# Edge ranks from TensorE products in place of 20 scans, and tiles 0 to 3 normed on their own, in the first block of a graph-transformer kernel

## The reference

```python
xn = layernorm(x)
W = einsum('rb,bio->rio', comp, basis)            # 8 relation matrices out of 4 bases
H = einsum('ni,rio->nro', xn, W)                  # rows of h_table
agg = segment_sum(H[src, etypes], dst, 2500)      # message passing
out = agg + xn @ loop_weight + bias
q, k, v = split(xn @ Wqkv.T + bqkv)               # and then an attention of its own
```

## Time and profile before

| | |
|---|---|
| median of 3 runs | 2431.36 us (2429.86 to 2431.77) |
| the profiled execution, first to last instruction | 2432.3 us |
| TensorE busy | 2103.5 us (86%) |
| VectorE busy | 1491.2 us (61%) |
| GpSimd busy | 974.7 us (40%) |
| ScalarE busy | 737.7 us (30%) |
| mean granted TensorE clock | 0.952 of full |
| first block, `slots_and_dense` | 0 to 138.6 us |
| second block, `front0` | 139.8 to 391.9 us |

### The profile page before, as it was taken

How to read it: one execution, slowest core, us unless ns; L and a number is a source line. 1 busy time by engine, 2 the same in 40 slices (tenths; PEclk the granted TensorE clock), 3 DMA queues, 4 the chain that set the end, 5 groups by cost and what they waited for, 6 DMA issues and landing times. The chain is left out here.

```text
span 2432.3 us, 31951 instructions
## 1 busy us (share of the span) xinstructions
PE 2103.5 (86%) x9692; PEld 1341.8 (55%) x9692; DVE 1491.2 (61%) x2938; ACT 737.7 (30%) x1962; POOL 974.7 (40%) x976
## 2 busy tenths in 40 slices
PE   4869996888899898699959958888887889999999
PEld 2346663444444446566636536666666766565665
DVE  8997777777787865433345558888887761211211
ACT  2511111111111113033312245555554232323232
POOL 4900004777666650055540067777776320000000
PEclk9989998999999998599979979999999989999999
DMA  3012223333333353433341178888888300000000
GB/s 113 31 59 98 98 93 95 103 102 102 95 94 95 94 75 102 156 53 57 57 102 44 44 210 243 240 239 239 239 240 199 113 1 1 9 9 1 9 9 8
DMA packets 118886, 241.54 MB, mean 99 GB/s; under 512 B 23255, under 2 KB 73182, under 8 KB 116030
## 3 DMA queue, kind: packets, MB, share of 16 engines
q0 software_dynamic: 56640, 160.17, 25.3%
q1 hardware_dynamic: 62078, 79.33, 10.1%
HBM read 196.24 MB, written 43.19 MB: 98 GB/s over the span
## 5 line engine op out<-in xcount | busy, mean ns | idle before, releaser
L672 POOL DMA_INDIRECT rows<-h_table,row_rel x372 | 361.4, 971 | 409.3 <-POOLq L95 268.1
L2137 PE MATMUL p_ag<-rows_g,oh_g 128*128 128x260 f32 x1488 | 398.7, 408 | 77.7 <-issue 57.6
L1980 POOL DMA_INDIRECT rows_g<-g_table,row_src x372 | 352.8, 949 | 255.1 <-POOLq L95 142.1
L2137 PEld LDWEIGHTS p_ag<-rows_g,oh_g 128*128 128x128 f32 x1488 | 256.9, 192 | 107.7 <-issue 74.3
L2503 DVE SCALAR_TENSOR_TENSOR x<-p_yf,cw_f,x 128x256 f32<-128x256 f32 (+1 forms) x160 | 66.4, 477 | 278.6 <-PE p_yf L2663 278.6
L927 PE MATMUL p_agg<-rows,oh 128*128 128x256 f32 x744 | 194.9, 396 | 24.8 <-DVE x L723 24.8
L2030 DVE TENSOR_TENSOR rows_g<-rows_g,p_e 128x2048 f32<-128x2048 f32 x93 | 211.8, 2278 | 0.0
L927 PEld LDWEIGHTS p_agg<-rows,oh 128*128 128x128 f32 x744 | 131.5, 190 | 88.6 <-DVE x L723 41.9
L792 DVE TENSOR_TENSOR fT<-a_sb,p_sel 128x512 f32<-128x512 f32 x200 | 128.6, 684 | 74.5 <-ACT a_sb L888 43.0
L2663 PE MATMUL p_yf<-f,h_f 128*128 128x256 f32 (+1 forms) x640 | 145.7, 381 | 0.8 <-ACT h_f L2555 0.8
L2613 PE MATMUL p_1f<-qT,f 128*128 128x512 f32 (+1 forms) x320 | 143.2, 591 | 0.5 <-ACT qT L2531 0.5
(11 more groups left out here) (434 smaller groups left out, 3535.8 us busy)
## 6 DMA issues: line engine op xcount, KB each, us to landing
h_table<-h_out SPq DMA_DIRECT2D x20, 1024.0 KB, 4.2
where_g<-d_table SPq DMA_DIRECT2D x93, 128.0 KB, 4.3
w<-in_L_ffn_W SPq DMA_DIRECT2D x16, 512.0 KB, 8.8
rows<-h_table,row_rel POOLq DMA_INDIRECT x372
rows_g<-g_table,row_src POOLq DMA_INDIRECT x372
g_table<-row SPq DMA_DIRECT2D x20, 260.0 KB
f<-in_L_ffn_W SPq DMA_DIRECT2D x16, 256.0 KB, 5.9
xT_table<-xT SPq DMA_DIRECT2D x20, 128.0 KB, 1.7
```

The lines of the kernel that those rows point to most:

```text
L672: pool.indirect_dma_start(rows[:, r, j], None, st.h_rows, bass.IndirectOffsetOnAxis(ap=st.row_rel[:, at:at + 1], axis=0)).then_inc(gathere ...
L1980: pool.indirect_dma_start(rows[:, r, j], None, st.g_table, bass.IndirectOffsetOnAxis(ap=st.row_src[:, at:at + 1], axis=0)).then_inc(gather ...
L2137: last = pe.matmul(p_a[:, k % NS, h, 0:HALF], oh[:, r, j], rows[:, r, j, h * HALF:(h + 1) * HALF], start=j % SUP == 0, stop=j % SUP == SUP ...
```

## The change

The loads are put in another order: x's first group, dst, the weights, then the other edge numbers and the rest of x. Tiles 0 to 3 are normed alone; the others follow after the edge work. `hot` is written by 20 instructions in place of one. The rank of an edge within its tile and column comes from a TensorE product with a triangle of ones (`before`, with 49152 on its diagonal, so that the edge's own tile has the largest value), to which a second product adds the start of that tile and column (`spread` times `start_h`). VectorE takes the maximum over the 20 tiles (`pos`). Counts come from 20 products (`count`), prefix sums over tiles from one (`prefix`, now at t = 3). The 32 instructions on `w_rel` stand between the maxima. GpSimd builds the constants for that, and its 20 additions of `b_v` to v go to the second block.

```diff
+MARK = 49152.0
+SPREAD = 32 + T
+CQ = T - 1
+PREFIX_AT = 3
+TILES_AT = 5
...
+            load_x(0)
+            sp.dma_start(dst_i[:, :], io["dst"].rearrange("(p c) -> p c", p=EP)).then_inc(dst_in, 16)
+            sp.dma_start(w_lv[:, :, 0:D], io["L0_gnn_loop_weight"].rearrange("(k p) o -> p k o", p=P)).then_inc(w_in, 16)
+            sp.dma_start(w_lv[:, :, D:], io["wqkv0"][:, 2 * D:].rearrange("(k p) o -> p k o", p=P)).then_inc(w_in, 16)
+            sp.dma_start(w_qk[:, :, :], io["wqkv0"][:, 0:2 * D].rearrange("(k p) o -> p k o", p=P)).then_inc(w_in, 16)
             sp.dma_start(src_i[:, :], io["src"].rearrange("(p c) -> p c", p=EP)).then_inc(edges_in, 16)
             sp.dma_start(et_i[:, :], io["edge_type_8"].rearrange("(p c) -> p c", p=EP)).then_inc(edges_in, 16)
-            for g in range(NG - 1):
-                sp.dma_start(st.x[:, g * GT * D:(g + 1) * GT * D].rearrange("p (t d) -> p t d", d=D),
-                             io["x"][g * GT * P:(g + 1) * GT * P, :].rearrange("(t p) d -> p t d", p=P)).then_inc(x_in[g], 16)
+            for g in range(1, NG - 1):
+                load_x(g)
...
+            pool.affine_select(out=spread[:, :, :], in_=spread[:, :, :], compare_op=ALU.not_equal, fill=1.0,
+                               base=0, pattern=[[-1, T], [0, EP]], channel_multiplier=1).then_inc(made, 1)
+            pool.wait_ge(made, 8)
+            pool.affine_select(out=spread[:, :, :], in_=spread[:, :, :], compare_op=ALU.not_equal, fill=float(SUP * P),
+                               base=-32, pattern=[[-1, T], [0, EP]], channel_multiplier=1).then_inc(spread_made, 1)
...
+            pool.wait_ge(b_in, 16)
+            for t in range(T):
                 pool.wait_ge(lv_used, t + 1)
-                pool.wait_ge(xn_ready, t + 1)
                 x = st.x[:, t * D:(t + 1) * D]
                 pool.tensor_tensor(x, x, loop_p[:, t % 2], ALU.add).then_inc(loop_added, 1)
-                v = v1_t[:, :, t * (DH + 1):t * (DH + 1) + DH]
-                pool.tensor_tensor(v, v, b_v[:, :].rearrange("p (h e) -> p h e", h=H), ALU.add).then_inc(v_added, 1)
-
-            def add_qk(t):
                 pool.wait_ge(qk_used, t + 1)
                 part = qk_t[:, :, t * DH:(t + 1) * DH]
-                pool.tensor_tensor(part, part, b_qk[:, :].rearrange("p (g e) -> p g e", g=2 * H), ALU.add).then_inc(v_added, 1)
-
-            pool.wait_ge(w_in, 80)
-            for t in range(T):
-                add_lv(t)
-                add_qk(t)
+                pool.tensor_tensor(part, part, b_qk[:, :].rearrange("p (g e) -> p g e", g=2 * H), ALU.add).then_inc(qk_added, 1)
...
+            norm(0, GT)
+            dve.wait_ge(dst_in, 16)
+            link(dve.tensor_scalar(e_i[:, :], dst_i[:, :], 7, None, ALU.logical_shift_right))
+            scaled(0, GT, 1)
+            link.inc(dve.tensor_scalar(dst_i[:, :], dst_i[:, :], P - 1, None, ALU.bitwise_and))
+            link(dve.tensor_copy(e_tile[:, :], e_i[:, :]))
+            for t in range(T):
+                last = dve.tensor_scalar(hot[:, t], e_tile[:, :], float(t), None, ALU.is_equal)
+                if t % GT == GT - 1:
+                    last.then_inc(tile_hot_ready, 1)
+
+            dve.wait_ge(edges_in, 32)
...
+            norm(GT, T)
+            scaled(GT, T, 2)
...
-            link(dve.tensor_tensor(hot[:, :, :], e_tile[:, :].unsqueeze(1).broadcast_to([EP, T, EC]),
-                                   iota_t[0:EP, :].unsqueeze(2).broadcast_to([EP, T, EC]), ALU.is_equal))
-            link(dve.tensor_reduce(tcount[:, :], hot[:, :, :], AX, ALU.add))
-            dve.sem_inc(counted, 1)
...
+            count = p_c[0:SPREAD, 0:EC]
+            dve.wait_ge(counted, 1)
+            link(dve.tensor_reduce(tcount[:, :], count, AX, ALU.add))
+            link(dve.tensor_scalar(need_i[:, :], tcount[:, :], float(SUP * P - 1), None, ALU.add))
             link(dve.tensor_scalar(need_i[:, :], need_i[:, :], 8, None, ALU.logical_shift_right))
             link(dve.tensor_copy(need[:, :], need_i[:, :]))
-            link(dve.tensor_tensor_scan(cum[:, :], ones_t[:, :], need[:, :], 0.0, ALU.mult, ALU.add))
-            link(dve.tensor_tensor(cum[:, :], cum[:, :], need[:, :], ALU.subtract))
-            link(dve.tensor_scalar(base[:, :], cum[:, :], float(SUP * P), -1.0, ALU.mult, ALU.add))
-            link(dve.tensor_tensor(base[0:EP, :], base[0:EP, :], p_t[0:EP, 1, 0:T], ALU.add))
-
-            link(dve.tensor_tensor(cmp_s, cum[0:1, :].unsqueeze(1).broadcast_to([1, NSUP, T]),
-                                   sup_i[:, :].unsqueeze(2).broadcast_to([1, NSUP, T]), ALU.is_le))
-            link(dve.tensor_reduce(tos[:, :], cmp_s, AX, ALU.add))
-            link(dve.tensor_scalar(st.tile_of[:, 0:NSUP], tos[:, :], -1.0, None, ALU.add))
-
+            dve.sem_inc(need_ready, 1)
+            link.inc(dve.tensor_tensor_scan(scan[:, :], ones_e[:, :], count, 0.0, ALU.mult, ALU.add))
+            dve.wait_ge(prefixed, 1)
+            link.inc(dve.tensor_copy(cum[:, :], p_s[0:SPREAD, 0:1]))
+            link(dve.tensor_scalar(base[:, :], p_s[0:SPREAD, 0:1], float(SUP * P), None, ALU.mult))
+            link.inc(dve.scalar_tensor_tensor(out=start_i[:, :], in0=scan[:, :], scalar=base[:, 0:1], in1=count, op0=ALU.add, op1=ALU.subtract))
+            link(dve.tensor_scalar(begun[:, :], st.iota_s[0:T, 0:NSUP], cum[0:T, 0:1], None, ALU.is_ge))
+            dve.sem_inc(begun_ready, 1)
+            link.inc(dve.tensor_scalar(start_i[0:32, :], start_i[0:32, :], SUP * P - 1, None, ALU.bitwise_and))
+            link(dve.tensor_scalar(start_i[32:, :], start_i[32:, :], 8, None, ALU.logical_shift_right))
+            link(dve.tensor_copy(start_h[:, :], start_i[:, :]))
+            dve.sem_inc(start_ready, 1)
...
+            dve.wait_ge(tiles_found, 1)
+            dve.tensor_scalar(st.tile_of[:, 0:NSUP], p_c[0:1, 0:NSUP], -1.0, None, ALU.add).then_inc(tiles_taken, 1)
+            dve.wait_ge(basis_in, 16 * (NB + 2))
+            done = 0
             for t in range(T):
-                link.inc(dve.tensor_tensor_scan(scan[:, t], ones_e[:, :], hot[:, t], base[0:EP, t:t + 1], ALU.mult, ALU.add))
-            dve.wait_ge(dv, link.base + link.k)
-            link(dve.tensor_tensor(scan[:, :, :], scan[:, :, :], hot[:, :, :], ALU.mult))
-            link(dve.tensor_reduce(e_a[:, :], scan[:, :, :].rearrange("p t c -> p c t"), AX, ALU.add))
-            link(dve.tensor_copy(dst_i[:, :], e_a[:, :]))
+                dve.wait_ge(slots_put, t + 1)
+                if t == 0:
+                    link.inc(dve.tensor_copy(pos[:, :], p_s[0:EP, 0:EC]))
+                else:
+                    link.inc(dve.tensor_tensor(pos[:, :], pos[:, :], (p_s, p_c)[t % 2][0:EP, 0:EC], ALU.max))
+                dve.wait_ge(dv, link.base + link.k)
+                dve.sem_inc(slots_taken, 1)
+                if t % 2:
+                    for n in range(done, done + 3):
+                        relation(n)
+                    done += 3
+            link(dve.tensor_scalar(dst_i[:, :], pos[:, :], -MARK, None, ALU.add))
...
-                link.inc(dve.tensor_tensor_scan(scan[:, t], ones_e[:, :], hot[:, t], base[0:EP, t:t + 1], ALU.mult, ALU.add))
-            dve.wait_ge(dv, link.base + link.k)
-            link(dve.tensor_tensor(scan[:, :, :], scan[:, :, :], hot[:, :, :], ALU.mult))
-            link(dve.tensor_reduce(e_a[:, :], scan[:, :, :].rearrange("p t c -> p c t"), AX, ALU.add))
...
+            def count():
+                pe.wait_ge(consts, NCONST)
+                for t in range(T):
+                    if t % GT == 0:
+                        pe.wait_ge(tile_hot_ready, t // GT + 1)
+                    last = pe.matmul(p_c[0:SPREAD, 0:EC], col_at[:, CQ - t:CQ - t + SPREAD], hot[:, t], start=t == 0, stop=t == T - 1)
+                last.then_inc(counted, 1)
...
+            def tiles():
+                pe.wait_ge(begun_ready, 1)
+                pe.wait_ge(start_ready, 1)
+                pe.matmul(p_c[0:1, 0:NSUP], ones_e[0:T, 0:1], begun[:, :], start=True, stop=True).then_inc(tiles_found, 1)
+
+            def put(t):
+                if t >= 2:
+                    pe.wait_ge(slots_taken, t - 1)
+                elif t:
+                    pe.wait_ge(tiles_taken, 1)
+                out = (p_s, p_c)[t % 2][0:EP, 0:EC]
+                pe.matmul(out, before[0:EP, 0:EP], hot[:, t], start=True, stop=False)
+                pe.matmul(out, spread[:, t], start_h[:, :], start=False, stop=True).then_inc(slots_put, 1)
...
+                if t == 1:
+                    count()
                 if t == PREFIX_AT:
                     prefix()
+                if t == TILES_AT:
+                    tiles()
+                    pe.wait_ge(spread_made, 1)
+                if TILES_AT <= t < TILES_AT + T // 2:
+                    put(2 * (t - TILES_AT))
+                    put(2 * (t - TILES_AT) + 1)
...
+        @block.gpsimd
+        def _(pool):
+            pool.wait_ge(st.b_v_in, 16)
+            for t in range(T):
```

(70 more changed lines are left out.)

128 lines of the change are left out of this document (62 added, 66 removed).

## The result

The changed kernel runs in 2414.4 us (median of 4 runs, 2409.39 to 2417.55), the kernel before in 2431.6 beside it: ratio 0.9924, 95% interval 0.9911 to 0.9938, 17 us. Repeated on another chip, with six runs, it is 0.9904 [0.9887, 0.9921], 22 us. The forecast was 2409, 22 us under; the first measurement lies 5.4 us above it, inside 2404 to 2416. The profiled execution was the fastest of its four, with a span of 2407.7 (clock 0.958), 24.6 under the span before.

The account below looks back on a forecast made before the run. VectorE was taken to end the first block, TensorE's 3.66 us per tile being the next bound; 33.8 us gained less 11.8 lost in `front0` gives 22.0, so 2409 us (2404 to 2416, 53%), with bounds 2393 to 2419.

Parts of the forecast that it names:

- the first block's gain: First block: `front0` starts at 106.0 in place of 139.8, 33.8 us earlier.
- the loss in `front0`: Second block: moved v additions and a slow clock make it 11.8 us later; bounds nothing and 14.
- TensorE from 11.5: First block: x lands at 6.5, `rstd` of tiles 0 to 3 at about 10, TensorE's tile 0 from 11.5.
- `hot` complete at 23, written in 12 us: First block: GpSimd's constants hold up the 20 `hot` rows, complete at 23 (bounds 14.5, 28), written in 12 rather than 4.4.
- need_ready at 34, TensorE there at 33: First block, ahead of tile 3: VectorE is ready 11 us behind `hot`, at 34; TensorE's tiles 1 and 2 end at 33.
- The rest, 68.7: First block: 17 tiles x 3.66, ten pairs of puts x 0.6, about 0.5 extras: 68.7 us, TensorE done at 103.
- Behind TensorE, GpSimd's last qk addition; VectorE idle from about 93: First block's end: GpSimd's addition to qk is last, at about 105; VectorE is idle from about 93 until then.
- hots(0) in turns, 18.5: Start of `front0`: GpSimd's 20 v additions alternate with VectorE's first 20 `hots` instructions, which take 18.5 us.
- rival "no turns": In `front0`, comparisons keep GpSimd out: loss 0 to 2 us, time 2398; chance 20%.
- 2.7 us for a slow clock: In `front0`, after TensorE's idle gap, 5.4 us of products run at half the clock at first, adding 2.7 us.
- TensorE's clock as the way to a slower kernel: First block: waits for `slots_taken` leave tiles at 1.2 GHz, 3.65 us more each, 2471 with all 17; chance 3%.
- the outermost rivals: 2392: constants don't delay `hot` (10%), combined with no turns. Upper: selects of 4.7 each (12%), 2414, up to 2419.

Follow-up runs that it names:

- run 3: Changed kernel with GpSimd's two selects on `spread` behind tile 0's additions and `iota_h` behind tile 9's; ratio 0.9905 to the kernel before.
- run 6: Changed kernel, first select waiting for `recs_split`, given as VectorE's last edge-number copy was issued, and `iota_h` behind tile 9; ratio 0.9904 to the kernel before.
- run 9: Changed kernel, selects after `rec_lo` is written, `iota_h` behind tile 9, v additions in the first block (tiles 0 to 3 four tiles late); ratio 0.9846 to the kernel before.
- run 10: Changed kernel, selects after `rec_lo` is written, `iota_h` behind tile 9, each v addition in `front0` waiting for a one-hot group; 2397.25 us, ratio 0.9835 to the kernel before.
- run 1: Changed kernel with GpSimd's addition to v of tile t waiting for `front0`'s one-hot group t + 1; ratio 0.9867 to the kernel before.
- run 4: Changed kernel with 40 additions to v in `front0`: 20 that add `b_v`, 20 that subtract it; ratio 0.9924 to the kernel before.
- run 2: Changed kernel with the additions to v back in the first block and `b_v` loaded after `b_qk`; ratio 0.9878 to the kernel before.
- run 7: Changed kernel with run 6's placing of the constants and the additions to v back in the first block; ratio 0.9883 to the kernel before.

## Why the prediction was right, and where its steps were not

The total came out: 2409 forecast, a ratio of 0.991, between the two measurements. Two errors of the sum nearly cancel: the first block's gain was put 5.0 us too high, the loss in `front0` 3.4 too high, and 22.0 became 20.4. That they cancel is luck. By its steps:

- *TensorE from 11.5*: **wrong, 17.1**. x landed earlier than assumed (4.76, not 6.5). The prediction charged the constants to `hot`; they fell on the work ahead of it. It held one-input f16 and int32 operations at risk and let the seven small operations of the norm run free. The rows after show L312, L315 and `e_i` held for 9.1 us, and runs 3, 6, 9 and 10, with the constants elsewhere, show TensorE starting at 8.7 to 8.8. The Trainium skill ("SBUF — State Buffer", section "Who interferes with whom") names both kinds: an instruction with two SBUF inputs against a GpSimd instruction that reads, and one in a two-port mode against any; with one input outside these modes there is no contention. The traces agree: two-input `mean` is held by a select, and one-input statistics go on at 0.33 beside one (run 6). Whether the held one-input operations (L315, `e_i`) ran in a two-port mode no trace shows.
- *`hot` complete at 23, written in 12 us*: complete at 20.3, written in 3.23, so this sign of being right did not come. TensorE did not wait, as it was late itself. The price of a select (2.2) was 2.47.
- *need_ready at 34, TensorE there at 33*: 32.5 and 33.8, no wait. The times are right, the way to them is not. In the forecast TensorE started at 11.5 and then stood from 17.7 to 23 for `hot`, 5.3 us. In fact it started 5.6 us later and never stood. The constants cost about what the forecast took them to cost (6.6 us at tile 3; runs 6, 9 and 10, without them, start front0 5.6 to 6.2 us earlier), through another wait; that the two are equal is luck. The 10 us for tiles 1 and 2 were 10.5: two tiles of 3.7 at the full clock and 3.1 for the count, where the prediction speaks of a slow clock.
- *The rest, 68.7*: **mis-sized, 74.2**. A pair of puts was priced at 0.6 from the 0.16 of `p_rec` products, and measured 1.15, ten times: 5.5 us, all of the first block's error. The number of products was right, their price was not: up to 0.29 for 340 columns, twice that of the count's of the same width.
- *Behind TensorE, GpSimd's last qk addition; VectorE idle from about 93*: right (109.87; 94.07).
- *hots(0) in turns, 18.5*: right in kind, 16.4 in size; comparisons go at 0.66 each, not 0.75. The clock near 0.5 as `p_rec` starts came too (0.50 from 124 to 127.5). Runs 1 and 4 settle it: without additions 3.93 for 17, with 40 the second group is as slow as the first. The rival "no turns" is out.
- *2.7 us for a slow clock*: 1.4 (6.96 against 5.54). TensorE's 9.0 us of idleness cost that much in this execution; it cost 2.0 in the repeat (7.54).
- *TensorE's clock as the way to a slower kernel*: it did not come; no put waited for `slots_taken`, and the clock stood at 1.00 from 41 to 108.
- *Slips in the working*, none of which moves the total: the select's own figures (0.17 and 0.9 ns a column) give 2.4 for 2500 columns, not 2.2; the slow-clock rival adds 3.65 us a tile, where the prediction's own tile of 6 us would add 2.3; and the outermost rivals, 2392 and 2420, lie 1 us outside the range given.

## What to carry to other kernels

When GpSimd and VectorE overlap, list every VectorE instruction in that stretch, small ones first, before deciding which is delayed: two operations of a norm chain on four columns and one in its midst took 9 us beside three constants, while statistics beside a select did not notice. Moving work off a full engine is free only where the receiver's neighbour has slack; 12.6 us of additions cost 8.4 in a place where VectorE was first in the chain, and nothing in the block from which they were taken (run 2), as long as they kept out of the norm chains (run 7). Price a handful of matmuls between others by such a handful, not by a run of 20 or 34 with the same columns.
